# Loads of x^T and stores of the output issued by ACT instead of SP, in an attention over 4096 memory slots

## The chip, the cores and the metric

One core of a Trainium2 chip runs the whole program in one launch. The metric is the device time in microseconds. An engine here is PE (TensorE, matrix products), DVE (VectorE), ACT (ScalarE), POOL (GpSimd) or SP (SyncE, which only issues transfers). ACT can issue transfers too, on a queue of its own.

## The reference, cut to what matters

`x` is 8192 tokens of 128 numbers. The first layer attends to a memory of 4096 slots, the second is a gated feed-forward block with 512 hidden columns.

```
q      = x @ Wq.T + bq
scores = q @ keys.T / sqrt(128)                 # 8192 x 4096
probs  = softmax(scores)
attn   = (probs @ values) @ Wo.T + bo
x1     = layernorm(x + attn)
h      = silu((x1 @ w1.T) * s1) * ((x1 @ w2.T) * s2)
h      = gelu((h @ h1.T) * sh1)
h      = gelu((h @ h2.T) * sh2)
out    = layernorm(x1 + (h @ w3.T) * s3)
```

The keys, values and the updated memory of the attention layer are not returned; only `out` is.

## The kernel before, in words

**Pairs and frames.** The attention takes the tokens in 32 pairs (`PAIRS`) of tiles of 128 rows. Time is cut into frames, one per pair: `frames` writes out the first four and the last four, and a loop of two frames per pass runs twelve times for the 24 between. Each engine has its own function `frame(f, par)`, whose steps `t` (16 per frame, on PE, ACT and POOL) or `j` (8 per frame, on DVE and SP) set the order of its work; between engines only semaphores order anything. One step `j` is two steps `t`.

**One pair's way.** PE projects q of pair f+1 at t = 8 of frame f (`q_project`, L951, from the buffer `x_in`, which holds x^T of one pair). ACT and DVE turn it into a high and a low part (`q_high_part` L592, `q_low_part` L762). PE makes the scores of a tile, 512 slots a step, with three products of high and low parts (L998 to L1000). DVE moves each piece of 1024 scores from PSUM to `rows` and takes its maximum (L812); ACT takes the exponential in place (`exp_piece`, L613); DVE transposes blocks of 32 by 32 in place (L779). Then SP sends the piece over to `slot_p`, so that the slots come to lie on the partitions: `send` (L377) has four DMAs for a piece, each from 32 partitions to 32, of 4 KB each. A pair has 8 pieces, so 32 DMAs of 128 KB. That is the **exchange**.

**Behind the exchange.** From t = 14 of the next frame on, 16 steps long, ACT rounds the probabilities to 16 bit (`high_part`, L622) and POOL makes the low part (L542), into a ring of 8; the first high part of a pair waits for all eight pieces of its exchange (L620). PE multiplies them with the values (`add_values`, L972 to L977), from the frame after. So pair f-2's values run beside pair f's scores.

**What SP does in a frame.** `slot_p` has room for two pairs: SP may begin pair f's exchange (piece 5 in the frame, `j` = 5) when POOL has done the low parts of pair f-2. In front of each piece it waits for DVE's transposition. Between the pieces it sends two more DMAs: behind piece `j` = 3 it stores the output sum of pair f-3 (`store_output`, L249: `o_sum` to `o_scratch`, 128 partitions of 1 KB), and behind `j` = 6 it waits until q of pair f+1 is projected and loads x^T of pair f+2 into `x_in` (L447, 128 partitions of 1 KB).

```
exchange(p, par if j > PIECES else 1 - par, tile, k)
if j == 3 and valid(f - 3, PAIRS):
    stage.store_output(sp, f - 3)
if j == 6 and valid(f + 2, PAIRS):
    sp.wait_ge(q_projected, f + 2)
    load_x(f + 2)
```

**What ACT does in a frame.** A high part in each of the 16 steps, the exponential of a piece in every second one, q's high part at t = 8, the first half of the output sum at t = 1 (L238). From frame 3 to 27 it also loads 226 columns of the feed-forward weights at t = 3 (L650, 113 KB, on its own queue) and rounds them at t = 13 (L653). DVE makes the output sum early in the frame (L244), when the store before it has landed.

**Behind the attention** the feed-forward block takes 16 blocks of 512 tokens; SP loads `o_scratch` and `x` for it and stores the result. The last three stores of output sums stand there, in SP's code behind its frames.

Of the kernel before, what the change touches and what calls it, by code (L numbers as in the profile page):

```python
# [27 lines left out]
P = 128  # L28
# [7 lines left out]
PAIRS = TOKENS // (2 * P)  # L36
# [40 lines left out]
def is_step(index, step):  # L77

    return isinstance(index, int) and index == step
# [9 lines left out]
def valid(index, end):  # L89

    return not isinstance(index, int) or 0 <= index < end
# [160 lines left out]
def layers(nc, stage, hold, xT, wqT, bq, kT, vT, woT, bo, scale_cols, w_raw, den, keys, rows, out_rows):  # L252
# [6 lines left out]
    def sb(name, shape, dt):  # L259
        return ctx.enter_context(nc.sbuf_tensor(name, shape, dt))  # L260
# [7 lines left out]
    x_in = sb("x_in", [P, 2 * P], FP32)  # L268
# [25 lines left out]
    x_loaded, q_projected, q_high, q_split = map(sem, ("x_loaded", "q_projected", "q_high", "q_split"))  # L294
# [28 lines left out]
    def turned_piece(f, j):  # L323


        if j == 0:
            return f - 1, 0, PIECES - 1
        if j <= PIECES:
            return f - 1, 1, j - 1
        return f, 0, j - PIECES - 1  # L330

    def part_step(f, t, lag):


        return (f - 1, t - lag) if t >= lag else (f - 2, t + STEPS - lag)

    def value_halves(f, t):


        step = t - V_STEP + STEPS * f if isinstance(f, int) else -1  # L340
        return (step,) if 0 <= step < HALVES else ()

    def checking(f):

        return not isinstance(f, int) or 0 <= f - FIRST_CHECK < CHECKS
# [97 lines left out]
    def _(sp):  # L443
        def load_x(pair):
            if is_step(pair, 1):
                sp.wait_ge(warmed, 1)
            sp.dma_start(x_in[:, :], xT[:, bass.ds(pair * 2 * P, 2 * P)]).then_inc(x_loaded, 16)  # L447

        load_x(0)
        sp.dma_start(wq[:, :], wqT).then_inc(wq_loaded, 16)  # L450
# [14 lines left out]
        def exchange(p, pp, tile, k):  # L465


            sp.wait_ge(turned, 8 * p + 4 * tile + k + 1)
            if tile == 0 and k == 0:
                if is_step(p, 1):  # L470
                    sp.wait_ge(v_split, HALVES)
                    sp.wait_ge(k_split, K_PARTS)
                at_least(sp, split, 16 * p - 16)
            send(sp, pp, tile, k)

        def frame(f, par):
            for j in range(2 * PIECES):
                p, tile, k = turned_piece(f, j)
                if valid(p, PAIRS):
                    exchange(p, par if j > PIECES else 1 - par, tile, k)  # L480
                if j == 3 and valid(f - 3, PAIRS):
                    stage.store_output(sp, f - 3)
                if j == 6 and valid(f + 2, PAIRS):
                    sp.wait_ge(q_projected, f + 2)
                    load_x(f + 2)

        frames(sp, frame)

# [98 lines left out]
    def _(act):  # L587
# [36 lines left out]
        def frame(f, par):  # L624
            for t in range(STEPS):
                p, s = part_step(f, t, T_LAG)
                if valid(p, PAIRS):
                    high_part(p, 1 - par if t >= T_LAG else par, s)
                if t == 8 and valid(f + 1, PAIRS):
                    q_high_part(f + 1, 1 - par)  # L630
                if t % 2 == 0:
                    tile, k = (1, t // 2) if t < 8 else (0, (t - 8) // 2)
                    if valid(f - tile, PAIRS):
                        exp_piece(f - tile, tile, k)
                if is_step(f, 0) and t == 9:
                    act.wait_ge(v_sum_ready, 1)
                    nc.scalar.activation(wo_size, wo, ACT.Abs, scale=v_sums[:, PIECES:]).then_inc(wo_sized, 1)
                for n in value_halves(f, t):
                    act.wait_ge(v_made, n + 1)
                    nc.scalar.activation(half_piece(v_hi_flat, n), o_ps[:, n % 2, :], ACT.Copy).then_inc(v_high, 1)  # L640
                    if n == 0:
                        act.wait_ge(k_split, K_PARTS)
                    nc.scalar.activation(half_piece(v_raw, n), o_ps[:, n % 2, :], ACT.Copy).then_inc(v_copied, 1)
                if t == 1 and valid(f - 3, PAIRS):
                    if is_step(f, 3):
                        act.wait_ge(unscale_ready, 1)
                    stage.output_half(act, f - 3, 1 - par)
                if t == 3 and checking(f):
                    at_least(act, w_rested, f - FIRST_CHECK)
                    act.dma_start(w_check, w_raw[:, bass.ds((f - FIRST_CHECK) * CHECK_COLS, CHECK_COLS)]).then_inc(check_loaded, 16)  # L650
                if t == 13 and checking(f):
                    act.wait_ge(check_loaded, 16 * (f - FIRST_CHECK) + 16)
                    nc.scalar.activation(check_part(f), w_check, ACT.Copy).then_inc(stage.w_rounded, 1)  # L653
                if is_step(f, PAIRS - 4) and t == 0:
                    for b in range(2):
                        act.wait_ge(stage.o_stored, 16 * 2 * (b + 1))
                        stage.load_o(act, b, b)
# [523 lines left out]
```

## Time and profile before

| | |
|---|---|
| median of 3 runs | 1123.45 us (1122.45 to 1124.76) |
| the profiled execution | 1123.78 us |
| its span | 1122.1 us |
| PE busy | 1081.3 us, 96% of the span |
| DVE busy | 968.3 us, 86% |
| ACT busy | 905.3 us, 81% |
| POOL busy | 642.1 us, 57% |
| exchange DMAs (L377) issued by SP | 1016 of 128 KB, median 2.4 us to landing |
| loads of x^T (L447) and stores of the sum (L249) | 32 and 32 of 128 KB, median 2.4 and 2.1 us |

Busy is the time in which an engine works on an instruction; issuing a DMA or waiting doesn't count. The attention fills the span to about 750 us, and the feed-forward block the rest. The DMA engines are busy for eight or nine tenths in the attention and for one tenth behind it. TensorE's granted clock is full but for the first and a middle stretch of a few microseconds.

### The profile page before, as it was taken

The page shows a single profiled execution, that of the slowest core. Times are in us where ns is not written, and L with a number is a line of the kernel's source. Part 1 is how long each engine was busy: PE and PEld are TensorE (multiplying, and loading weights), DVE is VectorE, ACT ScalarE, POOL GpSimd, SP SyncE. Part 2 cuts the span into 40 slices and gives each one's busy share as a digit, 9 for nine tenths or more (in the row PEclk, how much of TensorE's full clock was granted, in tenths as well). Part 3 has the DMA queues.
Part 4 walks back from the last instruction along what each step waited for, and adds up shares of the span by engine and source line. Part 5 has one row for each costly group of instructions (what it writes and reads, how often), then busy time and mean ns, then how long its engine had stood idle before and what let it go on. Part 6 is the DMA issues. An engine that isn't in the chain of part 4 may idle for free.

```text
span 1122.1 us, 20046 instructions
## 1 busy us (share of the span) xinstructions
PE 1081.3 (96%) x5324; PEld 770.6 (69%) x5324; DVE 968.3 (86%) x1806; ACT 905.3 (81%) x1609; POOL 642.1 (57%) x615
## 2 busy tenths in 40 slices
PE   7899999999999999999999999979999999999996
PEld 5666666666666666666666666636888888888875
DVE  6988998998899989988999899887788887888884
ACT  6788788788888887888888878788788888878883
POOL 0487788788888787878887888760211121121110
PEclk9999999999999999999999999999999999999999
DMA  6888888988889889898898988891011011011000
GB/s 207 199 192 197 198 198 205 208 198 201 209 201 205 200 204 207 199 200 209 200 209 198 212 200 188 192 262 53 1 56 29 28 53 31 28 29 55 11 12 27
DMA packets 83941, 165.89 MB, mean 148 GB/s; under 512 B 19648, under 2 KB 47808, under 8 KB 83776
## 3 DMA queue, kind: packets, MB, share of 16 engines
q1 hardware_dynamic: 79632, 160.97, 60.4%
q10 hardware_dynamic: 4272, 4.47, 1.5%
q8 instruction: 18, 0.29, 0.1%
q14 instruction: 19, 0.16, 0.0%
HBM read 22.76 MB, written 8.39 MB: 28 GB/s over the span
## 4 chain that ended last, share of the span: by engine, by line
PE 36%; SPq 15%; ACT 13%; issue 10%; DVE 9%; POOL 8%; DMA 7%; ACTq 1%; DVEq 0%; POOLq 0%
SPq L377 14%; PE ring L1045 12%; PE ring L1046 12%; POOL pT L542 7%; ACT rows L613 7%; DMA slot_p<-rows 6%; ACT pT L622 5%; DVE rows L812 3%; DVE rows L779 3%; PE o_ps L1045 1%; PE o_ps L1046 1%; PE s_ps L1000 1%; PE s_ps L998 1%; PE s_ps L999 1%; PE o_ps L972 1%
## 5 line engine op out<-in xcount | busy, mean ns | idle before, releaser
L542 POOL TENSOR_TENSOR pT<-slot_p,pT 128x512 f16<-128x512 f32 x482 | 545.7, 1166 | 130.5 <-ACT pT L622 130.5
L622 ACT ACTIVATE pT<-slot_p 128x512 f16<-128x512 f32 x512 | 296.5, 617 | 72.5 <-DMA slot_p<-rows 60.3
L812 DVE TENSOR_SCALAR_CACHE_REDUCE rows<-s_ps 128x1024 f32<-128x1024 f32 x256 | 308.6, 1205 | 51.8 <-DMA slot_p<-rows 34.7
L779 DVE STREAM_TRANSPOSE rows<-rows 128x1024 f32<-128x1024 f32 x256 | 316.7, 1238 | 9.2 <-ACT rows L613 5.4
L613 ACT ACTIVATE rows<-rows,bias 128x1024 f32<-128x1024 f32 x256 | 291.7, 1140 | 12.6 <-DVE bias L820 12.0
L998 PE MATMUL s_ps<-keys,q_buf 128*128 128x512 f32 x512 | 249.6, 487 | 6.0 <-DVE rows L812 4.0
L972 PE MATMUL o_ps<-pT,v_hi 128*128 128x512 f16 x512 | 197.5, 386 | 18.5 <-POOL pT L542 11.2
L1000 PE MATMUL s_ps<-keys,q_buf 128*128 128x512 f32 x512 | 202.5, 396 | 0.0
L999 PE MATMUL s_ps<-keys,q_buf 128*128 128x512 f32 x512 | 201.3, 393 | 0.0
L975 PE MATMUL o_ps<-pT,v_lo 128*128 128x256 f16 x1024 | 196.1, 273 | 0.0
L977 PE MATMUL o_ps<-pT,v_hi 128*128 128x512 f16 x512 | 194.6, 380 | 0.0
L164 POOL TENSOR_TENSOR var_eps<-moments,eps 128x4 f32<-128x4 f32 x32 | 6.4, 199 | 312.8 <-DVE moments L185 312.8
L975 PEld LDWEIGHTS o_ps<-pT,v_lo 128*128 128x128 f16 x1024 | 101.1, 99 | 84.2 <-issue 0.6
L1045 PE MATMUL ring<-keys,w_all 128*128 128x512 f32 x384 | 153.3, 399 | 1.0 <-ACT gate L669 0.9
L1046 PE MATMUL ring<-keys,w_all 128*128 128x512 f32 x384 | 150.5, 392 | 0.0
L694 ACT ACTIVATE gelu<-ring,scales 128x512 f32<-128x512 f32 x128 | 87.8, 686 | 59.1 <-PE ring L1046 59.1
L972 PEld LDWEIGHTS o_ps<-pT,v_hi 128*128 128x128 f16 x512 | 49.3, 96 | 108.0 <-POOL pT L542 49.0
L998 PEld LDWEIGHTS s_ps<-keys,q_buf 128*128 128x128 f32 x512 | 97.0, 189 | 25.1 <-DVE rows L812 4.9
L1000 PEld LDWEIGHTS s_ps<-keys,q_buf 128*128 128x128 f32 x512 | 96.3, 188 | 22.7
L999 PEld LDWEIGHTS s_ps<-keys,q_buf 128*128 128x128 f32 x512 | 97.0, 189 | 17.5
L876 DVE TENSOR_TENSOR h_lo<-gelu,h_hi 128x512 fp32r<-128x512 f32 x128 | 81.9, 688 | 26.5 <-ACT h_hi L698 26.3
L1045 PE MATMUL ring<-h_hi,w_all 128*128 128x512 f32 x256 | 103.1, 403 | 0.3 <-ACT gate L669 0.3
(98 smaller groups left out, 1327.2 us busy)
## 6 DMA issues: line engine op xcount, KB each, us to landing
slot_p<-rows SPq DMA_DIRECT2D x1016, 128.0 KB, 2.4
x_in<-in_xT SPq DMA_DIRECT2D x32, 128.0 KB, 2.4
x_in<-in_x SPq DMA_DIRECT2D x16, 256.0 KB, 3.5
o_scratch<-o_sum SPq DMA_DIRECT2D x32, 128.0 KB, 2.1
out<-y_out SPq DMA_DIRECT2D x16, 256.0 KB, 2.4
o_in<-o_scratch SPq DMA_DIRECT2D x14, 256.0 KB, 3.2
z<-in_w_all ACTq DMA_DIRECT2D x25, 113.0 KB, 2.7
rows<-in_w_all SPq DMA_DIRECT2D x1, 2816.0 KB, 12.9
```

The source lines that it names most:

```text
L542: nc.gpsimd.tensor_tensor(halves(s % RING, 1), slots_first(pp, s), halves(s % RING, 0), ALU.subtract).then_inc(split, 1)
L613: nc.scalar.activation(s, s, ACT.Exp, bias=bias[:, tile:tile + 1], scale=SCALE, accum_out=den[:, bass.ds((2 * p + tile) * PIECES + k, 1)]) ...
L622: nc.scalar.activation(halves(s % RING, 0), slots_first(pp, s), ACT.Copy).then_inc(highed, 1)
L779: nc.vector.transpose(row_piece(tile, k), row_piece(tile, k)).then_inc(turned, 1)
L812: nc.vector.tensor_scalar(row_piece(tile, k), s_ps[:, j % 2, :], 1.0, None, ALU.mult, ALU.max, accum_out=part_max[:, tile, k:k + 1]).then_ ...
L972: nc.tensor.matmul(o_ps[:, pp, :], v_hi[:, 2 * s, :], pT[:, s % RING, 0, :], start=s == 0, stop=False, skip_group_check=True)
L975: nc.tensor.matmul(o_ps[:, pp, 0:2 * P], v_lo[:, 2 * s + c, :], pT[:, s % RING, c, 0:2 * P], start=False, stop=False, skip_group_check=True)
L998: nc.tensor.matmul(out, q_h, k_h, start=True, stop=False)
L999: nc.tensor.matmul(out, q_h, k_l, start=False, stop=False)
L1000: last = nc.tensor.matmul(out, q_l, k_h, start=False, stop=True)
L1045: nc.tensor.matmul(out, wh, hh, start=n == 0, stop=False)
L1046: last = nc.tensor.matmul(out, wh, hl, start=False, stop=final and not low_weights)
```

## The change

The two DMAs leave SP's frame and stand in ACT's, at t = 13: behind that step's high part, in front of the rounding of the weights' columns and of t = 14, where the first high part of a pair waits for its exchange. ACT waits for what SP waited for: `o_ready` for the store (inside `store_output`), `q_projected` for the load. SP keeps the first two loads of x^T and the last three stores of the sum.

```diff
@@ block.sync, load_x
-            sp.dma_start(x_in[:, :], xT[:, bass.ds(pair * 2 * P, 2 * P)]).then_inc(x_loaded, 16)
+            sp.dma_start(x_in[:, :], xT[:, pair * 2 * P:(pair + 1) * 2 * P]).then_inc(x_loaded, 16)
@@ block.sync, frame
                     exchange(p, par if j > PIECES else 1 - par, tile, k)
-                if j == 3 and valid(f - 3, PAIRS):
-                    stage.store_output(sp, f - 3)
-                if j == 6 and valid(f + 2, PAIRS):
-                    sp.wait_ge(q_projected, f + 2)
-                    load_x(f + 2)
@@ block.scalar, frame
+                if t == 13 and valid(f - 3, PAIRS):
+                    stage.store_output(act, f - 3)
+                if t == 13 and valid(f + 2, PAIRS):
+                    act.wait_ge(q_projected, f + 2)
+                    act.dma_start(x_in[:, :], xT[:, bass.ds((f + 2) * 2 * P, 2 * P)]).then_inc(x_loaded, 16)
                 if t == 13 and checking(f):
                     act.wait_ge(check_loaded, 16 * (f - FIRST_CHECK) + 16)
                     nc.scalar.activation(check_part(f), w_check, ACT.Copy).then_inc(stage.w_rounded, 1)
```

The order of SP's instructions in the second frame of the loop's body, behind piece `j` = 3, before. `x4` are the four DMAs of a piece; REGISTER_ALU and ISA rows work out what a wait compares with or where a DMA goes.

```order
L249 ISA
L249 DMA o_scratch<-o_sum 128x256
L468 REGISTER_ALU
L377 DMA slot_p<-rows 32x1024 x4
L468 ISA
L86 ISA
L377 DMA slot_p<-rows 32x1024 x4
L468 REGISTER_ALU
L377 DMA slot_p<-rows 32x1024 x4
L484 REGISTER_ALU
L447 ISA
L447 DMA x_in<-in_xT 128x256
```

The same place now, from piece `j` = 3 to the loop's branch:

```order
L377 DMA slot_p<-rows 32x1024 x4
L468 REGISTER_ALU
L377 DMA slot_p<-rows 32x1024 x4
L468 ISA
L86 ISA
L377 DMA slot_p<-rows 32x1024 x4
L468 REGISTER_ALU
L377 DMA slot_p<-rows 32x1024 x4
L468 REGISTER_ALU
L377 DMA slot_p<-rows 32x1024 x4
L368 REGISTER_ALU
L368 COMPARE_AND_BRANCH
```

SP's pieces follow each other with nothing between them.

ACT's instructions around t = 13 and 14 of a frame in the loop, now (the lines of the changed file are 5 lower than before up to this place: L617 is the high part L622, L608 the exponential L613):

```order
L608 ACTIVATE rows,den<-rows,bias 128x1024
L86 REGISTER_ALU
L617 ACTIVATE pT<-slot_p 128x2x256
L249 ISA
L249 DMA o_scratch<-o_sum 128x256
L650 ISA
L650 DMA x_in<-in_xT 128x256
L653 REGISTER_ALU
L653 ACTIVATE w_all<-z 128x226
L615 REGISTER_ALU
L86 ISA
L617 ACTIVATE pT<-slot_p 128x2x256
```

The two DMAs stand behind the sixteenth high part of one pair and in front of the wait (L615) of the first of the next. No other engine's order changes.

## Rows read from the trace of the kernel before

**Rows 1.** One frame: PE, PEld, DVE, ACT, POOL busy (count), clock, DMA share, GB/s.

```profile
401.37:423.54 22.17, 22.17 (x116) 15.14 (x115) 20.48 (x31) 18.73 (x35) 18.93 (x18) 1.00 0.87 199
```

**Rows 2.** ACT's timeline, q's conversion: start, duration, instruction, [idle before <- releaser].

```profile
83.87 0.48 ACT L592 ACTIVATE q_buf<-x_ps,bq_col 128x256 fp32r<-128x256 f32 x1 [1.76 <-PE x_ps L951]
...
221.18 0.47 ACT L592 ACTIVATE q_buf<-x_ps,bq_col 128x256 fp32r<-128x256 f32 x1 [1.30 <-PE x_ps L951]
...
401.37 0.47 ACT L592 ACTIVATE q_buf<-x_ps,bq_col 128x256 fp32r<-128x256 f32 x1 [1.31 <-PE x_ps L951]
...
423.54 0.47 ACT L592 ACTIVATE q_buf<-x_ps,bq_col 128x256 fp32r<-128x256 f32 x1 [1.62 <-PE x_ps L951]
...
446.28 0.47 ACT L592 ACTIVATE q_buf<-x_ps,bq_col 128x256 fp32r<-128x256 f32 x1 [1.28 <-PE x_ps L951]
...
626.30 0.47 ACT L592 ACTIVATE q_buf<-x_ps,bq_col 128x256 fp32r<-128x256 f32 x1 [1.29 <-PE x_ps L951]
...
695.84 0.48 ACT L592 ACTIVATE q_buf<-x_ps,bq_col 128x256 fp32r<-128x256 f32 x1 [1.22 <-PE x_ps L951]
```

**Rows 3.** PE's timeline, the held-up values' matmul.

```profile
436.70 0.39 PE L972 MATMUL o_ps<-pT,v_hi 128*128 128x512 f16 x1 [0.50 <-POOL pT L542]
```

**Rows 4.** POOL's and ACT's timelines: waits before low and first high parts.

```profile
425.88 5.65 POOL L542 TENSOR_TENSOR pT<-slot_p,pT 128x512 f16<-128x512 f32 x5 [1.59 <-ACT pT L622]
...
433.13 0.63 ACT L622 ACTIVATE pT<-slot_p 128x512 f16<-128x512 f32 x1 [2.70 <-DMA slot_p<-rows]
...
454.97 0.63 ACT L622 ACTIVATE pT<-slot_p 128x512 f16<-128x512 f32 x1 [1.69 <-DMA slot_p<-rows]
```

**Rows 5.** The chain of waits, 405 to 435 us: start, duration, what.

```profile
411.19 0.59 SPq L377
...
411.89 0.53 SPq L377
...
430.61 2.34 DMA slot_p<-rows
```

**Rows 6.** The page's chain by line; SP's waits in all (us, times, longest).

```profile
SPq L377 14%; PE ring L1045 12%; PE ring L1046 12%; POOL pT L542 7%; ACT rows L613 7%; DMA slot_p<-rows 6%; ACT pT L622 5%; DVE rows L812 3%; DVE rows L779 3%; PE o_ps L1045 1%; PE o_ps L1046 1%; PE s_ps L1000 1%; PE s_ps L998 1%; PE s_ps L999 1%; PE o_ps L972 1%
...
SPq L377 <- POOL pT L542: 15.2, 18, 1.3
```

**Rows 7.** SP's timeline, 405 to 430 us.

```profile
405.67 8.66 SPq L377 DMA_DIRECT2D slot_p<-rows  x12
414.58 0.36 SPq L447 DMA_DIRECT2D x_in<-in_xT  x1
415.06 12.95 SPq L377 DMA_DIRECT2D slot_p<-rows  x20
428.30 0.36 SPq L249 DMA_DIRECT2D o_scratch<-o_sum  x1
428.77 1.79 SPq L377 DMA_DIRECT2D slot_p<-rows  x3
```

**Rows 8.** ACT's timeline with its queue's issue, 414 to 418 us.

```profile
414.38 0.34 ACTq L650 DMA_DIRECT2D z<-in_w_all  x1
...
416.44 1.14 ACT L622 ACTIVATE pT<-slot_p 128x512 f16<-128x512 f32 x2
```

**Rows 9.** DMA views of 428:436, 440:445, 414:418; queues (packets, MB, share), issues (landing).

```profile
q1 hardware_dynamic: 696, 1.62, 87.6%
slot_p<-rows SPq DMA_DIRECT2D x13, 128.0 KB, 2.3
...
q1 hardware_dynamic: 394, 1.07, 100.4%
slot_p<-rows SPq DMA_DIRECT2D x9, 128.0 KB, 3.4
...
q10 hardware_dynamic: 144, 0.12, 11.2%
```

**Rows 10.** Line 377's issues by ACT: duration min/median/max in ns.

```profile
L377 ACTq DMA_DIRECT2D slot_p<-rows x8: 601/818/1352, 737.8 to 744.4; - x8
```

## The prediction

> **What bounds the kernel now.** I first read one frame of the loop as a window between two of ACT's conversions of q. From 401.37 to 423.54 us PE is busy for all of its 22.17 us at the full clock, while DVE, ACT and POOL are busy for 18.7 to 20.5 us [rows 1]. So a frame costs at least 22.17 us, and what can be won is only what stands above that. The starts of the conversions of q give the pace [rows 2]: 22.17 us from 401.37, but 22.74 us from 423.54. Over 18 frames, from 221.18 to 626.30, two frames take 405.12 / 9 = 45.01 us, against 2 x 22.17 = 44.34: **0.67 us per two frames is above PE's pace**.
>
> Where PE loses it stands in PE's timeline: the values' matmul of 436.70 was held up for 0.50 us by POOL's low part (L542) [rows 3]. Who held POOL up? POOL's first low part of a pair follows ACT's first high part (L622) at 433.13, and that had waited 2.70 us for the exchange to land [rows 4]. The exchange's last DMA was issued at 430.61 and took 2.34 us to land [rows 5]. So the path is: SP's queue of 32 exchange DMAs, a landing, ACT, POOL, PE. The chain of waits gives SP's exchange 14% of the span, more than any other line [rows 6].
>
> How full is SP? Twenty exchange DMAs take 12.95 us, 0.65 each, as do others whatever else runs [rows 7]. Beside the 32 of a pair, SP sends one load of x^T and one store. Between pairs SP is free: in all it waits 15.2 us in 18 places for POOL, 1.3 us at most [rows 6]. That wait ends by PE's own pace, not by SP's: POOL sat idle for 1.59 us for ACT at 425.88, and ACT for 1.62 us for PE's q at 423.54 [rows 2, 4]. So what SP saves inside a pair's exchange brings its end forward, and isn't handed on to the next start.
>
> **The change, part by part.**
>
> *Taken from SP.* The load: the exchange ends an issue at 405.67 + 8.66 = 414.33 and begins the next at 415.06, a hole of 0.73 us. The store: 415.06 + 12.95 = 428.01 to 428.77, 0.76 us [rows 7]. Between two groups of exchange DMAs with nothing between them the hole is 411.89 - (411.19 + 0.59) = 0.11 us [rows 5]. The load is therefore worth 0.62 and the store 0.65: **1.27 us per pair**, both ahead of the DMA that ACT's first high part waits for. That is 0.60 more than the 0.67 that PE lacks.
>
> *Given to ACT.* Two issues, 0.36 and 0.36 to 0.42 us on SP [rows 7], with two waits that were met long ago: the sum of output f-3 was made at the start of the same frame, and the projection of q is what ACT converted five steps before. I cost them at nothing, for two reasons. ACT idles 2.70 us right behind that place (1.69 in the other frame of a body) [rows 4]. And ACT's queue issues ahead of its arithmetic: the DMA of the weights' columns went out at 414.38, though it stands in the program between the two conversions that run from 416.44, so at least 2 us ahead [rows 8]. If that cover went, the price would be some 1.1 us, issued from 430.43, still over before a landing at about 432.
>
> *New: two queues at once.* The moved DMAs now lie in ACT's queue, leaving 2 to 5 us before SP's last exchange DMA, and their 256 KB share the DMA engines with the exchange. Before, they stood in SP's own queue and the exchange paid for them with a slot. The price is the least certain term. Nearest rows: while SP is alone its exchange DMAs land in 2.3 us and fill 87.6% of the engines; some microseconds behind the weights' DMA on ACT's queue they land in 3.4 us, and the engines are full at 100.4% [rows 9]. So one DMA of 113 KB can cost 1.1 us. The bounds for two moved ones are 0 (SP no later than alone) and 2 x 1.1 = 2.2 us. By engine time, the 113 KB took 11.2% of 4 us = 0.45 us [rows 9], so 256 KB take 1.02; with 12% of the engines free for some 4 us about 0.5 is left when the last DMA goes out, with none free all 1.02. I take 0.8 us, between the two and nearer the full state, since twice as much arrives at once as in that row.
>
> A rule of the Trainium skill, in DMA: Bandwidth & Descriptors, section Issuing engines are not separate DMA queues, speaks against the change: DMAs of all issuers run on the same 16 engines, and a second issuer saves only the sequencer's time, usually small beside the DMA. By that rule, the gain is the 1.27 us of issue at best and no data moves faster; the trace agrees with the first half, and here issue is no small part, since 32 slots of 0.65 us nearly fill the frame.
>
> *Not moved.* PE, DVE and POOL keep their order. The bytes are the same. The store leaves within some 3 us of where it did (428.30) and only has to land before the next frame's sum. x^T is loaded some 10 us earlier, just behind the projection that frees its buffer, and is needed a frame later. Both stay hidden. The stores of the last three pairs stay with SP.
>
> *The sum.* The last exchange DMA leaves 1.27 us earlier and lands 0.8 later: 0.47 us of the 0.67 come back, and 0.20 stay, as the wait of PE for POOL.
> - Nine loop bodies from 221.18 to 626.30: 9 x 0.47 = 4.2 us.
> - The six frames from 83.87 to 221.18 take 137.31 us, 4.29 over PE's pace [rows 2]. Entering the loop is in it; I take half, 2.1 us.
> - The three frames from 626.30 to 695.84 take 69.54 us, 3.03 over [rows 2]. DVE has the first block's residual there; I take a third, 1.0 us.
> - Behind that SP's stores mostly stay: nothing.
>
> In all 7.3 us. The profiled execution took 1123.78 us; 1123.78 - 7.3 = 1116.5. The median shown is 0.33 below that execution, so 1116.2 against it; I write **1116.5**.
>
> **The rivals.**
>
> *All of the stall goes.* If the late landing is 0.6 us or less, the 1.27 covers the 0.67. Then 9 x 0.67 = 6.0, three quarters of the 4.29 (3.2) and half of the 3.03 (1.5): 10.7 us, 1113. For it: by engine time it can be 0.5, and SP now rests longer between pairs, so that each exchange starts on empty engines. Against it: the 3.4 us behind a single 113 KB DMA.
>
> *It lands as late as it leaves early.* At 1.27 us, just over the 1.1 of the one measured burst, nothing is left: 1123. Another road to the same is that ACT, not the exchange, begins the pair late, but the 2.70 us of idle time speak against that.
>
> *Slower: the two queues hold the exchange back more than its slots did.* The place is the last four exchange DMAs of a pair, right behind the burst, and the point from which it decides is 1.27 us of added time. At the bound of 2.2 us PE would wait 2.2 - 0.60 = 1.6 us per body in place of 0.67: 0.93 x 12 bodies = 11 us, 1135. A milder form is that issues slow each other: near 740 us, where ACT and SP both send the exchange, ACT's eight issues took 601 to 1352 ns against the usual 590 [rows 10]. If ACT's two issues took 0.4 us each from SP, 0.8 of the 1.27 would be gone; with 0.8 of late landing PE would wait 1.0, 0.33 more than now, x 12 = 4 us, 1128. Against that: the weights' single issue of 0.34 us runs beside SP's, whose slots stay 0.65 [rows 7, 8]. By Perfetto Trace Analysis in the Trainium skill, section DMA Instruction — HWDGE (DVE, Sync), issuers take a lock on one generator of descriptors, and the wait for it is part of an issue's time; by that the milder form would hold for each of the two issues.
>
> *The change doesn't reach the path*, because SP only waits longer for POOL: 1123. That holds for what it saves between pairs, but the two slots stand inside the pair.
>
> **How the numbers follow.** A measurement of this kernel can tell about 0.2%, 2.2 us, from no change. My forecast (0.5 to 1.0 us of late landing) has 0.38, all of the stall gone 0.28: faster 0.66. Landing as late as it leaves early 0.14 and not reaching the path 0.06: same 0.20. Slower 0.14, most of it in the milder form. The range goes from 1111.5, a little beyond all of the stall gone, to 1125, which leaves out the larger part of the slower case: about 5% below and 12% above.
>
> **What would show it.** Right: between conversions of q 22.2 us in nearly every frame; PE's wait for POOL's L542 at most 0.3 us per body; no hole in SP's exchange inside a pair, and SP's waits for POOL between pairs longer by over 1 us each; ACT's two DMAs some microseconds ahead of its first high part; exchange DMAs behind them landing in about 3.1 us. Wrong: slots of SP above 0.65 us beside ACT's issues; landings of 3.6 us or more at the end of a pair with the pace still at 45 us per two frames; or PE's stall unchanged though the exchange lands over 1 us earlier, which would make ACT or POOL the holder, not SP.

## The result, and the profile after

Five runs of the kernel before have a median of 1124.06 us (1122.45 to 1124.76), five of the changed kernel one of 1117.74 us (1116.99 to 1118.10). The ratio is 0.9937 (95%: 0.9926 to 0.9949): the change makes the kernel faster by 0.63%, three times the 0.2% that the prediction took for the least a measurement can tell. 1116.5 was predicted, with a range that holds the measured time. The profiled execution took 1118.10 us, against 1123.78 before.

The head of the page after. The span is 5.7 us shorter; no engine has less to do by more than 2.4 us, so what went is mostly waiting:

```profile
span 1116.4 us, 20012 instructions
PE 1078.9 (97%) x5324; PEld 770.3 (69%) x5324; DVE 972.3 (87%) x1806; ACT 903.0 (81%) x1609; POOL 642.2 (58%) x615
```

**Where the time went** is read from ACT's timeline after, at the conversions of q that answer to [rows 2] (L587 is L592 before). A body is one pass of the loop, two frames:

```profile
84.20 0.48 ACT L587 ACTIVATE q_buf<-x_ps,bq_col 128x256 fp32r<-128x256 f32 x1 [1.76 <-PE x_ps L951]
...
220.15 0.48 ACT L587 ACTIVATE q_buf<-x_ps,bq_col 128x256 fp32r<-128x256 f32 x1 [1.30 <-PE x_ps L951]
...
398.39 0.47 ACT L587 ACTIVATE q_buf<-x_ps,bq_col 128x256 fp32r<-128x256 f32 x1 [1.31 <-PE x_ps L951]
...
420.48 0.47 ACT L587 ACTIVATE q_buf<-x_ps,bq_col 128x256 fp32r<-128x256 f32 x1 [1.63 <-PE x_ps L951]
...
443.12 0.47 ACT L587 ACTIVATE q_buf<-x_ps,bq_col 128x256 fp32r<-128x256 f32 x1 [1.29 <-PE x_ps L951]
...
621.99 0.48 ACT L587 ACTIVATE q_buf<-x_ps,bq_col 128x256 fp32r<-128x256 f32 x1 [1.32 <-PE x_ps L951]
...
690.99 0.48 ACT L587 ACTIVATE q_buf<-x_ps,bq_col 128x256 fp32r<-128x256 f32 x1 [1.75 <-PE x_ps L951]
```

| stretch | before | after | saved | predicted |
|---|---|---|---|---|
| up to the first of these | 83.87 | 84.20 | -0.33 | 0 |
| six frames | 137.31 | 135.95 | 1.36 | 2.1 |
| eighteen frames (nine bodies) | 405.12 | 401.84 | 3.28 | 4.2 |
| three frames | 69.54 | 69.00 | 0.54 | 1.0 |
| behind | 426.26 | 425.41 | 0.85 | 0 |
| sum | | | 5.70 | 7.3 |

The same frames as windows after: PE, PEld, DVE, ACT, POOL busy (count), clock, DMA share, GB/s. Two frames of about 22.1 us stand beside one of 22.64, at full clock; [rows 2] had 22.17 and 22.74:

```profile
376.34:398.39 22.05, 21.90 (x114) 14.53 (x113) 20.62 (x32) 18.17 (x35) 17.96 (x18) 1.00 0.90 210
398.39:420.48 22.09, 22.09 (x116) 15.06 (x115) 20.25 (x30) 18.62 (x36) 18.94 (x18) 1.00 0.85 200
420.48:443.12 22.64, 22.32 (x116) 14.89 (x115) 20.84 (x34) 18.61 (x36) 18.36 (x18) 1.00 0.93 208
```

**SP.** Its timeline after, for the stretch of [rows 7]. The exchange DMAs, 32 of one pair and the first of the next, form one row with neither a load nor a store in it:

```profile
406.28 25.76 SPq L377 DMA_DIRECT2D slot_p<-rows  x38
```

**ACT.** Its timeline after. The two DMAs are issued at 421.76 and 422.31, though they stand in the program behind the high part of 426.33 (t = 13): 4.6 and 4.0 us ahead of it, and 4.5 and 3.9 us ahead of SP's last exchange DMA of that pair (426.25, below). The first high part waits 2.74 us, as it did before (2.70, [rows 4]). The exponential behind it follows with no gap:

```profile
421.76 0.37 ACTq L249 DMA_DIRECT2D o_scratch<-o_sum  x1
422.31 0.34 ACTq L650 DMA_DIRECT2D x_in<-in_xT  x1
...
426.33 0.62 ACT L617 ACTIVATE pT<-slot_p 128x512 f16<-128x512 f32 x1
426.85 0.38 ACT L653 ACTIVATE w_all<-z 128x226 f32 x1
429.96 0.63 ACT L617 ACTIVATE pT<-slot_p 128x512 f16<-128x512 f32 x1 [2.74 <-DMA slot_p<-rows]
...
430.50 1.14 ACT L608 ACTIVATE rows<-rows,bias 128x1024 f32<-128x1024 f32 x1
```

**The landing.** The chain of waits after, for the place of [rows 5], where the last exchange DMA took 2.34 us to land. It now takes 3.53:

```profile
425.62 0.59 SPq L377
426.25 3.53 DMA slot_p<-rows
```

The DMA view after of 423 to 427 us, queues as packets, MB, share of 16 engines, and the issues with their landing. ACT's queue holds 21.3% and SP's 77.9%, together 99.2%:

```profile
q1 hardware_dynamic: 284, 0.77, 77.9%
...
q10 hardware_dynamic: 288, 0.26, 21.3%
...
slot_p<-rows SPq DMA_DIRECT2D x7, 128.0 KB, 3.5
```

**PE.** Its timeline after: the matmul of [rows 3] waits 0.32 us instead of 0.50.

```profile
433.54 0.39 PE L972 MATMUL o_ps<-pT,v_hi 128*128 128x512 f16 x1 [0.32 <-POOL pT L537]
```

The waits between 221 and 622 us (us in total, times, longest), of the kernel before:

```profile
ACT pT L622 <- DMA slot_p<-rows: 39.6, 18, 2.7
PEld o_ps L972 <- POOL pT L542: 26.9, 75, 1.1
...
PE o_ps L972 <- POOL pT L542: 5.4, 9, 0.7
```

and of the changed kernel:

```profile
ACT pT L617 <- DMA slot_p<-rows: 40.7, 18, 2.8
...
PEld o_ps L972 <- POOL pT L537: 18.2, 56, 0.8
...
PE o_ps L972 <- POOL pT L537: 1.2, 4, 0.4
```

PE's matmuls wait for POOL 4 times in place of 9, 1.2 us in place of 5.4, and its weight loads 18.2 us in place of 26.9. ACT waits for the exchange as long as before: what SP no longer takes, the landing takes. In the whole span, SP's own wait for POOL grew:

```profile
SPq L377 <- POOL pT L537: 39.8, 24, 2.2
```

That is 24.6 us more than the 15.2 of [rows 6]: 1.27 us in some twenty pairs would be 25. (A second row of SP's waits for POOL, at line 86, has 6.3 us in 5 places before and 8.7 in 6 after.) What SP saves inside a pair it gives to the pause between pairs.

### The profile page after: what moved, and what is told of

The parts are those of the page before. It is cut to its first block, busy times and chain, and to the rows that moved or that the text cites. A ratio compares the mean times of both kernels' runs of the same rounds, so it can differ in the third digit from the quotient of the medians.

```text
span 1116.4 us, 20012 instructions
## 1 busy us (share of the span) xinstructions
PE 1078.9 (97%) x5324; PEld 770.3 (69%) x5324; DVE 972.3 (87%) x1806; ACT 903.0 (81%) x1609; POOL 642.2 (58%) x615
## 4 chain that ended last, share of the span: by engine, by line
PE 47%; issue 11%; ACT 10%; POOL 9%; DVE 8%; SPq 7%; DMA 6%; ACTq 1%; POOLq 0%; DVEq 0%
PE ring L1045 13%; PE ring L1046 12%; POOL pT L537 9%; SPq L377 7%; ACT rows L608 5%; DMA slot_p<-rows 5%; ACT pT L617 3%; PE s_ps L1000 3%; PE s_ps L998 3%; PE s_ps L999 3%; PE o_ps L972 3%; PE o_ps L975 3%; PE o_ps L977 3%; DVE rows L779 2%; DVE rows L812 2%
## 5 line engine op out<-in xcount | busy, mean ns | idle before, releaser
L617 ACT ACTIVATE pT<-slot_p 128x512 f16<-128x512 f32 x512 | 296.5, 617 | 75.2 <-DMA slot_p<-rows 70.5
L812 DVE TENSOR_SCALAR_CACHE_REDUCE rows<-s_ps 128x1024 f32<-128x1024 f32 x256 | 309.4, 1209 | 38.4 <-PE s_ps L1000 20.3
L608 ACT ACTIVATE rows<-rows,bias 128x1024 f32<-128x1024 f32 x256 | 291.6, 1139 | 5.5 <-DVE bias L820 5.3
```

What stands on the lines that cost most here:

```text
L608: nc.scalar.activation(s, s, ACT.Exp, bias=bias[:, tile:tile + 1], scale=SCALE, accum_out=den[:, bass.ds((2 * p + tile) * PIECES + k, 1)]) ...
L617: nc.scalar.activation(halves(s % RING, 0), slots_first(pp, s), ACT.Copy).then_inc(highed, 1)
L812: nc.vector.tensor_scalar(row_piece(tile, k), s_ps[:, j % 2, :], 1.0, None, ALU.mult, ALU.max, accum_out=part_max[:, tile, k:k + 1]).then_ ...
```

## The experiments

The theory to be tested: SP's 32 slots and what stands between them, the landing, ACT, POOL and PE form one path; ACT's issues cost nothing where they stand; the moved bytes cost the landing. All kernels were read in one way, by the timelines of SP and ACT. Each number is a mean over the seventeen pairs 10 to 26 of the loop: **start**, the first exchange issue behind the conversion of q ahead of it; **slots**, first to last exchange issue; **landing**, last issue to ACT's first high part; **path**, their sum; **pace**, us per frame. In eleven of the twelve kernels the high part starts 0.19 us behind the landing of the last exchange DMA, so that the column does tell of the landing. In g1_all_sp it doesn't, as its section shows.

| kernel | start | slots | landing | path | pace |
|---|---|---|---|---|---|
| before | 8.10 | 21.06 | 2.53 | 31.69 | 22.51 |
| after | 7.90 | 19.80 | 3.65 | 31.35 | 22.31 |
| e1_store | 8.50 | 20.42 | 3.13 | 32.05 | 22.62 |
| e2_load | 7.94 | 20.44 | 2.87 | 31.25 | 22.25 |
| e3_behind | 8.30 | 19.83 | 3.70 | 31.83 | 22.85 |
| e4_between | 7.88 | 19.82 | 2.77 | 30.47 | 22.08 |
| f1_small | 7.88 | 19.79 | 2.70 | 30.37 | 22.08 |
| f2_small_sp | 8.02 | 21.05 | 2.52 | 31.59 | 22.44 |
| f3_small_behind | 7.90 | 19.79 | 3.05 | 30.74 | 22.34 |
| f4_double | 7.89 | 19.94 | 4.03 | 31.86 | 22.51 |
| g1_all_sp | 8.41 | 19.83 | 3.53 | 31.77 | 22.47 |
| g2_store6 | 8.16 | 20.49 | 3.31 | 31.96 | 22.58 |

The runs f1_small, f2_small_sp and f3_small_behind leave out seven eighths of each store and load, so that their output isn't the reference's; they are for the time alone. The kernels of one letter ran on one chip, each against the kernel before on that chip: 1125.14 us (e), 1126.00 (f), 1125.45 (g).

### Only the store moved

```diff
@@ SP, frame
-                if j == 3 and valid(f - 3, PAIRS):
-                    stage.store_output(sp, f - 3)
@@ ACT, frame
+                if t == 13 and valid(f - 3, PAIRS):
+                    stage.store_output(act, f - 3)
```

> Only the store of the output sum moves to ACT at t = 13; the load of x^T stays between SP's pieces. Theory A (SP's slots are won inside a pair's exchange, and the moved DMAs' landing gives most of it back): the last exchange DMA of a pair leaves 0.65 us earlier (20.6 us behind the first in place of 21.25) and lands some 0.5 us later; a tenth of a microsecond per pair is left, 1121 to 1123.5 us. Rival B (the gain of the change is the store's alone, since it stood right ahead of the last piece): about 1118. Rival C (it is the load's alone): 1124, no change.

Measured: 1126.23 us, ratio 1.0009 (1.0000 to 1.0018). This is no gain, and none of the expected 1121 to 1123.5: a miss. Half of the slots' saving is there (20.42 in place of 21.06), but the landing takes back 0.60 of the 0.64, and the exchange starts 0.40 later. The time is what rival C forecast for this run.

### Only the load moved

```diff
@@ SP, frame
-                if j == 6 and valid(f + 2, PAIRS):
-                    sp.wait_ge(q_projected, f + 2)
-                    load_x(f + 2)
@@ ACT, frame
+                if t == 13 and valid(f + 2, PAIRS):
+                    act.wait_ge(q_projected, f + 2)
+                    act.dma_start(x_in[:, :], xT[:, bass.ds((f + 2) * 2 * P, 2 * P)]).then_inc(x_loaded, 16)
```

> Only the load of x^T moves to ACT at t = 13; the store stays between SP's pieces. Theory A: 0.62 us earlier, some 0.5 us later in landing, 1121 to 1123.5 us. Rival B (the store's alone): 1124, no change. Rival C (the load's alone): about 1118.

Measured: 1116.45 us, ratio 0.9919 (0.9904 to 0.9934). The load alone brings at least all of the gain. Theory A's 1121 to 1123.5 is missed here too; rival C's forecast of both runs was the nearest. Its reason, that a load is cheap and a store dear, is put to the test by the last experiment. The slots are as long as in the first experiment, but the landing is 2.87 and not 3.13, and the start is early. SP's timeline and ACT's show how: ACT's load leaves at 422.95, SP's store at 425.76, with the last piece's four exchange DMAs behind the store, and the high part waits only 2.04 us. The DMA views of 423.6 to 425.7 us and of 426.2 to 428.2 have the landings on either side of the store's place: 3.1 us ahead of it, 2.4 behind it.

```profile
403.63 21.84 SPq L377 DMA_DIRECT2D slot_p<-rows  x32
425.76 0.34 SPq L249 DMA_DIRECT2D o_scratch<-o_sum  x1
```

```profile
422.95 0.34 ACTq L650 DMA_DIRECT2D x_in<-in_xT  x1
...
430.60 0.63 ACT L619 ACTIVATE pT<-slot_p 128x512 f16<-128x512 f32 x1 [2.04 <-DMA slot_p<-rows]
```

```profile
slot_p<-rows SPq DMA_DIRECT2D x3, 128.0 KB, 3.1
...
slot_p<-rows SPq DMA_DIRECT2D x4, 128.0 KB, 2.4
```

### Both on ACT, behind its first high part

Against the changed kernel:

```diff
@@ ACT, frame
                     high_part(p, 1 - par if t >= T_LAG else par, s)
+                if t == 14 and valid(f - 3, PAIRS):
+                    stage.store_output(act, f - 3)
+                if t == 14 and valid(f + 2, PAIRS):
+                    act.wait_ge(q_projected, f + 2)
+                    act.dma_start(x_in[:, :], xT[:, bass.ds((f + 2) * 2 * P, 2 * P)]).then_inc(x_loaded, 16)
...
-                if t == 13 and valid(f - 3, PAIRS):
-                    stage.store_output(act, f - 3)
-                if t == 13 and valid(f + 2, PAIRS):
-                    act.wait_ge(q_projected, f + 2)
-                    act.dma_start(x_in[:, :], xT[:, bass.ds((f + 2) * 2 * P, 2 * P)]).then_inc(x_loaded, 16)
```

> Both DMAs on ACT, but behind the first high part of a pair (t = 14), so that they go out only when the pair's exchange has landed, near the next pair's start. Theory A: the last exchange DMA leaves 20.0 us behind the first as in the change, and now lands in 2.5 us again in place of 3.6; PE's wait for POOL's first low parts goes, q's conversions stand 22.1 us apart in every frame, 1110 to 1114 us. Rival D (what is left of PE's stall is ACT's or POOL's own, not the late landing): 1117 to 1119, with the landing at 2.5 us. Rival E (the burst does the same harm wherever it lies, since the exchange runs nearly without a gap): landing at 3.3 us or more at the pair's end, 1117 to 1120.

Measured: 1132.83 us, ratio 1.0065 (1.0052 to 1.0079), slower, and outside all three forecasts, none of which gave ACT's issues a price. Two things show. The landing is 3.70, as rival E said, though the burst now leaves at the beginning of an exchange and not near its end. And ACT's issues are in the way. Its timeline:

```profile
436.63 0.63 ACT L617 ACTIVATE pT<-slot_p 128x512 f16<-128x512 f32 x1 [1.70 <-DMA slot_p<-rows]
436.79 0.37 ACTq L249 DMA_DIRECT2D o_scratch<-o_sum  x1
437.33 0.35 ACTq L628 DMA_DIRECT2D x_in<-in_xT  x1
437.81 1.15 ACT L608 ACTIVATE rows<-rows,bias 128x1024 f32<-128x1024 f32 x1 [0.56 <-issue]
```

The exponential, which in the changed kernel ran on the heels of the high part, stands idle for 0.56 us for issue. A gap of 0.56 in each pair's round of two frames is 0.28 per frame; the pace of 22.85 lies some 0.34 above the 22.5 that other kernels have at a path of 31.7 to 31.9.

### Both on SP, where it waits for POOL anyway

Against the kernel before:

```diff
@@ SP, frame
             for j in range(2 * PIECES):
+                if j == 5 and valid(f - 3, PAIRS):
+                    stage.store_output(sp, f - 3)
+                if j == 5 and valid(f + 2, PAIRS):
+                    sp.wait_ge(q_projected, f + 2)
+                    load_x(f + 2)
                 p, tile, k = turned_piece(f, j)
                 if valid(p, PAIRS):
                     exchange(p, par if j > PIECES else 1 - par, tile, k)
-                if j == 3 and valid(f - 3, PAIRS):
-                    stage.store_output(sp, f - 3)
-                if j == 6 and valid(f + 2, PAIRS):
-                    sp.wait_ge(q_projected, f + 2)
-                    load_x(f + 2)
```

> Both DMAs stay on SP, but stand together in front of the first piece of a pair (j = 5), where SP waits for POOL's low parts. ACT issues nothing more than before. Theory A (only what lies between the first and the last exchange DMA counts, and SP has over 1 us to spare between pairs): 20.0 us from first to last, landing in 2.5 us, 1110 to 1115 us. Rival F (SP's issues in all are the bound, or the second queue is what helps): 1123 to 1125, as before. In between if the wait for POOL is shorter than the 1.27 us of the two slots, so that the first piece starts late.

Measured: 1111.99 us, ratio 0.9881 (0.9866 to 0.9896), the best of all the kernels that compute the whole. The slots are 19.82 as in the change, the landing is 2.77 (2.53 before), and the path falls by 1.22. So theory A holds and rival F is out. SP's timeline: both issues lie in the pause between two pairs, the 32 of a pair follow each other in 20.59 us.

```profile
401.43 0.42 SPq L249 DMA_DIRECT2D o_scratch<-o_sum  x1
402.13 0.35 SPq L447 DMA_DIRECT2D x_in<-in_xT  x1
402.98 20.59 SPq L377 DMA_DIRECT2D slot_p<-rows  x32
```

Its frames, with the columns of [rows 1]. PE is busy in all of both, in 21.99 and 22.17 us, so that 22.08 is what PE alone needs on the average; the 22.17 of [rows 1] was the longer kind of frame:

```profile
373.11:395.10 21.99, 21.99 (x116) 14.96 (x115) 20.23 (x30) 18.68 (x36) 18.68 (x18) 1.00 0.89 210
395.10:417.27 22.17, 22.17 (x116) 15.14 (x115) 21.01 (x33) 18.62 (x36) 18.65 (x18) 1.00 0.88 204
```

### The bytes or the issues?

Four kernels ask what makes the landing late. In the first three, the store and the load inside the frames move 16 partitions and not 128. The first is the changed kernel with this:

```diff
-        sp.dma_start(self.o_dram[:, bass.ds(p * 2 * P, 2 * P)], self.o_sum[:, :]).then_inc(self.o_stored, 16)
+        sp.dma_start(self.o_dram[0:16, bass.ds(p * 2 * P, 2 * P)], self.o_sum[0:16, :]).then_inc(self.o_stored, 16)
...
-                    act.dma_start(x_in[:, :], xT[:, bass.ds((f + 2) * 2 * P, 2 * P)]).then_inc(x_loaded, 16)
+                    act.dma_start(x_in[0:16, :], xT[0:16, bass.ds((f + 2) * 2 * P, 2 * P)]).then_inc(x_loaded, 16)
```

> The change, but every moved load and every store of the sum takes 16 partitions of 1 KB in place of 128 (the feed-forward block reads its attention part from x^T instead, so the output leaves the attention out): ACT issues as often, an eighth of the bytes. Theory G (it is the bytes on ACT's queue that make the exchange land late): the last exchange DMA leaves 20.0 us behind the first and lands in 2.6 to 3.0 us, as where SP sends both between the pairs; frames of 22.1 us, 1110 to 1113 us. Rival H (it is the issuing from a second queue as such, or ACT's time for it): landing at 3.3 us or more, 1116 to 1118.

Measured: 1111.99 us, ratio 0.9868 (0.9852 to 0.9884). As theory G said, the landing falls from 3.65 to 2.70 and the pace to PE's own 22.08.

The second is the kernel before, with the same small DMAs on SP:

```diff
-                sp.dma_start(x_in[:, :], xT[:, bass.ds(pair * 2 * P, 2 * P)]).then_inc(x_loaded, 16)
+                sp.dma_start(x_in[0:16, :], xT[0:16, bass.ds(pair * 2 * P, 2 * P)]).then_inc(x_loaded, 16)
```

> The kernel before, with the same loads and stores cut to 16 partitions, on SP in their old places. Theory I (on SP it is the slot that costs, not the bytes): 21.25 us from first to last exchange DMA as before, 1122 to 1125 us. Rival J (it is the bytes): landing at 2.3 us or less and frames of 22.1 us, 1112 to 1116. Between the two if a DMA of 16 partitions has a shorter slot.

Measured: 1121.99 us, ratio 0.9958 (0.9941 to 0.9975). The time is at the lower edge of theory I's range. The slots stay at 21.05, the landing at 2.52. On SP it is the two places in the queue that cost most; the bytes are worth 4.0 us by the medians, against the 13.2 that clearing both places brought in e4_between. On ACT it is the bytes.

The third is the kernel with both behind ACT's first high part, with small DMAs:

```diff
+                if t == 14 and valid(f + 2, PAIRS):
+                    act.wait_ge(q_projected, f + 2)
+                    act.dma_start(x_in[0:16, :], xT[0:16, bass.ds((f + 2) * 2 * P, 2 * P)]).then_inc(x_loaded, 16)
```

> Both DMAs on ACT behind the first high part, as in the slower run, but with 16 partitions. Theory K (that run lost time twice: 1 us by late landing at the pair's end, and 0.66 us because ACT's second high part of a pair waits behind two issues): now the landing is 2.6 to 3.0 us, and the first high part to PE's first values stays at 4.2 us against 3.6; together 1112 to 1118 us. Rival L (all of its loss was the late landing): 1110 to 1113, with 3.6 us from the first high part to PE's values.

Measured: 1118.10 us, ratio 0.9927 (0.9910 to 0.9943). The bytes are all but gone and the path is 30.74, yet the pace is 22.34 and not 22.08. The time lies 0.1 us above theory K's range and the landing of 3.05 just above its 3.0; rival L is out. What is left is ACT's issue time, in its timeline:

```profile
428.11 0.40 ACTq L249 DMA_DIRECT2D o_scratch<-o_sum  x1
428.68 0.35 ACTq L629 DMA_DIRECT2D x_in<-in_xT  x1
429.16 1.15 ACT L609 ACTIVATE rows<-rows,bias 128x1024 f32<-128x1024 f32 x1 [0.58 <-issue]
```

The first of the three has the same DMAs ahead of ACT's wait and not behind it, and is 6.1 us faster. The price of two issues without cover is 0.56 to 0.58 us of ACT, and about 0.26 us per frame.

The fourth is the changed kernel, with the store sent twice, the second time to a tensor that nobody reads:

```diff
         sp.dma_start(self.o_dram[:, bass.ds(p * 2 * P, 2 * P)], self.o_sum[:, :]).then_inc(self.o_stored, 16)
+        sp.dma_start(self.o_dram2[:, bass.ds(p * 2 * P, 2 * P)], self.o_sum[:, :]).then_inc(self.o_stored, 16)
```

> The change with every store of the sum sent twice, the second time to another buffer in memory: 384 KB per frame from ACT's queue at t = 13 in place of 256. Theory G: the last exchange DMA lands 0.3 to 0.6 us later still, about 4.0 to 4.3 us, 1120 to 1126 us. Rival M (lateness doesn't grow with the bytes, it is a state that any burst brings about): 3.6 us as in the change, 1117 to 1119.

Measured: 1124.92 us, ratio 0.9990 (0.9979 to 1.0002). The landing rises from 3.65 to 4.03, the slots from 19.80 to 19.94: 0.5 us more of path for 128 KB, and the gain is gone. From 32 KB on ACT's queue (2.70) to 256 (3.65) to 384 (4.03) the landing rises by 0.4 us per 100 KB and by 0.3. So the more is moved, the later the landing, and rival M is out. Bytes and packets grow together in these runs (the view of 423 to 427 us above has 288 packets for the 0.26 MB of ACT's two DMAs), so that they don't tell the one from the other. And here ACT's issues do slow SP's: in f4_double, the 56 of SP's exchange issues between 230 and 620 us that overlap one of ACT's store or load took 611 ns in the mean; in the changed kernel the 42 such issues took 575, as all of them there do.

### Everything on SP, and the store at another place

If a second queue is what delays the exchange, then it should run free with ACT's queue silent. This kernel is that with both on SP in the pause, and the weights' columns there as well:

```diff
@@ SP, frame, ahead of the store at j == 5
+                if j == 5 and checking(f):
+                    at_least(sp, w_rested, f - FIRST_CHECK)
+                    sp.dma_start(w_check, w_raw[:, bass.ds((f - FIRST_CHECK) * CHECK_COLS, CHECK_COLS)]).then_inc(check_loaded, 16)
@@ ACT, frame
-                if t == 3 and checking(f):
-                    at_least(act, w_rested, f - FIRST_CHECK)
-                    act.dma_start(w_check, w_raw[:, bass.ds((f - FIRST_CHECK) * CHECK_COLS, CHECK_COLS)]).then_inc(check_loaded, 16)
```

> Store, load and also the load of the weights' columns on SP, all three in front of the first piece of a pair (j = 5); ACT's queue issues nothing in the frames. Theory A: landing is 2.5 us at the end of every pair (it was 2.6 and 2.95 with the weights' columns on ACT's queue), but PE was already at its pace of 22.1 us per frame, so 1109 to 1113 us. Rival N (three slots are longer than SP's wait for POOL, so the exchange starts some 0.3 us late and PE waits again): 1114 to 1118.

Measured: 1123.29 us, ratio 0.9978 (0.9968 to 0.9988), outside both forecasts. The late start that the rival named is there (8.41 in place of 7.88). SP's timeline shows the three DMAs one behind the other, and the exchange directly behind them:

```profile
407.62 0.44 SPq L480 DMA_DIRECT2D z<-in_w_all  x1
408.27 0.36 SPq L249 DMA_DIRECT2D o_scratch<-o_sum  x1
408.90 0.34 SPq L447 DMA_DIRECT2D x_in<-in_xT  x1
409.48 20.59 SPq L377 DMA_DIRECT2D slot_p<-rows  x32
```

The 3.53 of the table look like a late landing, but aren't one. The DMA view of 409.5 to 430 us, which holds that exchange, gives the median of its 32 landings:

```profile
slot_p<-rows SPq DMA_DIRECT2D x32, 128.0 KB, 2.3
```

The last exchange DMA of a pair lands in 2.35 us on the average of the seventeen pairs, earlier than in e4_between (2.58): that part of theory A holds. ACT's timeline shows what the first high part (L625) waited for instead. In front of it in the program stands the rounding of the weights' columns (L653), and their load now leaves SP only at 430.33, behind the exchange's last issue, and no longer at t = 3, ten steps ahead of the rounding:

```profile
429.52 0.63 ACT L625 ACTIVATE pT<-slot_p 128x512 f16<-128x512 f32 x1
432.55 0.39 ACT L653 ACTIVATE w_all<-z 128x226 f32 x1 [2.40 <-DMA z<-in_w_all]
433.01 0.63 ACT L625 ACTIVATE pT<-slot_p 128x512 f16<-128x512 f32 x1
```

The same in the waits between 221 and 622 us, where no wait of L625 is left:

```profile
ACT w_all L653 <- DMA z<-in_w_all: 41.9, 18, 2.6
```

The high part comes 1.17 us behind the landing in place of 0.19, and this 0.98 is a wait that the edit itself made. Without it the path would be 31.77 - 0.98 = 30.79, and the pace about 22.04 by what the other kernels have (22.25 at 31.25, 0.46 per microsecond), which is PE's own; that is an estimate, no run has it. So 369 KB on SP's own queue just ahead of the exchange don't make it land late, where 256 KB on ACT's queue do (e3_behind).

The last kernel asks why the load alone did better than the store alone. It is the one that moved only the load, with SP's store not behind piece `j` = 3, near the end of an exchange, but behind `j` = 6, near its beginning:

```diff
-                if j == 3 and valid(f - 3, PAIRS):
+                if j == 6 and valid(f - 3, PAIRS):
                     stage.store_output(sp, f - 3)
```

> Load of x^T on ACT at t = 13 as in the run that gained most of the two single ones, and SP's store one position earlier in the pair's exchange: behind j = 6, where the load's slot was, in place of j = 3, right ahead of the last piece. Theory O (the slot of a short transfer in SP's queue right ahead of the last piece lets the DMA engines catch up, so that the last piece lands in 2.6 us in spite of ACT's burst): landing now 3.0 us or more, 1120 to 1126 us. Rival P (a load on ACT's queue is cheap and a store is dear, wherever SP's own stands): landing 2.6 to 2.9 us, 1115 to 1118.

Measured: 1124.81 us, ratio 0.9995 (0.9985 to 1.0005), against 0.9919 with the store at `j` = 3. The bytes, queues and counts are the same; the slots too (20.49 and 20.44). The landing is 3.31 in place of 2.87 and the start 8.16 in place of 7.94. So theory O holds and rival P is out. Here the eight exchange DMAs issued from 426 to 430.6 us, behind the burst and with no place between them, land in 3.0 us (median); in e2_load it was 3.1 ahead of the store and 2.4 behind it. A place in SP's queue that holds a short transfer lets the DMA engines catch up: it helps if it stands between the burst and the end of the exchange, and is wasted if it stands ahead of the burst.

## Why the prediction was right, and which term was off

**What bounds the kernel: held, with a floor 0.09 too high.** In the table, the pace follows the path: from 31.25 to 32.05 us of path it rises from 22.25 to 22.62, 0.46 us per frame for each microsecond (g1_all_sp is on this line too, since its path has ACT's wait for the weights' columns in it). A pair's path lies in a round of two frames, so one half is what it should be. At 30.4 us it stands at PE's 22.08, where that line would lie lower. Only the two kernels with ACT's issues behind the first high part lie off this line. Against 22.08, PE lacked 45.01 - 44.16 = 0.85 us per body and not 0.67.

**The slots taken from SP: 1.27 predicted, 1.26 measured** (21.06 - 19.80), and 24.6 us longer waits for POOL between pairs, as the prediction said. Its reading that SP waits for POOL 15.2 us in all, 1.3 at most, left out the row of line 86 (6.3 us, longest 1.9); nothing in the sum rests on it. That the saving stands inside the pair, and is worth something only there, is what the kernel with both on SP in the pause shows: the same slots, all of the gain. "The change doesn't reach the path" is out.

**ACT's issues at nothing: held.** The queue ran 4.0 and 4.6 us ahead of the arithmetic in front of it in the program; at least 2 had been expected. The cover is needed: without it the price is 0.56 us.

**The late landing: the term that was mis-sized.** 0.8 was taken, 3.65 - 2.53 = 1.12 us was measured. The prediction took engine time (1.02 us if no engine is free) and put it down a little for the 12% it thought free. With the view of 423 to 427 us at 99.2%, none was free. So the exchange alone gave 1.26 - 1.12 = 0.14 us per pair, not 0.47: at this point the rival "lands as late as it leaves early" was all but true.

**What made up for it was not foreseen.** The exchange starts 0.20 us earlier behind q (7.90 in place of 8.10). 0.14 + 0.20 is 0.34 us per body, and the nine bodies gave 3.28 / 9 = 0.36. The cause of the earlier start is argued and not shown: in the span's waits, DVE waited for its own rows' last landing (L812) 34.7 us before and 15.4 after, so that its pieces, which SP sends, are made sooner; in the loop alone (221 to 622 us) they are 19.2 before, 8.1 after and 25.1 in e1_store, whose exchange starts at 8.50. No run takes this alone. So the closeness of 1116.5 to 1117.74 is in part luck: a saving that the prediction had no term for made up for most of what the landing cost beyond 0.8. With 0.14 us per pair alone, its own sum would give 7.3 x 0.14 / 0.47 = 2.2 us, about 1121.6, still inside its range. Two of its signs of being right failed: only every second frame takes the 22.1 us that it wanted in nearly every one (22.09 and 22.64 stand side by side), and the exchange DMAs behind the burst land in 3.5 us, not 3.1. One of its signs of being wrong, 3.6 us or more with the pace still at 45 us per two frames, was near: the table's landing is 3.65, the pace 44.65.

**The other stretches** were estimated by shares and came to 1.36 and 0.54 in place of 2.1 and 1.0, about the same factor as in the loop. The 0.33 lost ahead of them and the 0.85 us behind the attention are not explained by any run. For the latter a candidate stands in the trace before: for the 3.4 us from 739.4 the granted clock was 0.50 (the lower level, 1.2 GHz), with PE busy for 3.18 of them. In the trace of the changed kernel it was 0.50 only at the very end, where PE was idle.

**The rivals.** "All of the stall goes" was put at 1113 and needed a landing under 0.6 us later. It didn't come, but f1_small and e4_between show that it was right about what would follow: 1111.99 both. "Slower: the two queues" had its place right and its size wrong: 1.12 us, not 2.2, stays below the 1.27 from which it decides, and f4_double, at 1.50 later with slots 0.14 longer, is just at the turn (0.9990). For its milder form, slots lengthened by ACT's issues, the kernel gives no support: line 377's issues on SP have a median of 591 ns after and 590 before, and the slots are 19.80 us beside ACT's two issues and 19.82 without them (e4_between). Only three of ACT's issues lengthened them, in f4_double, by 0.14. By Perfetto Trace Analysis in the Trainium skill, section DMA Instruction — HWDGE (DVE, Sync), ACT's issues and SP's would have to wait for one lock; if they do, it doesn't show in a median, two issues beside 32.

The rule of DMA: Bandwidth & Descriptors in the Trainium skill, section Issuing engines are not separate DMA queues, did hold: one set of DMA engines serves both queues, and the bytes moved to ACT came back as 1.12 us of landing, against 1.26 of issue time. What it calls usually small was 0.63 us for each of the two DMAs here.

**Still open.** Why a burst of about 1 us of engine time on ACT's queue still costs 0.9 us at the end of an exchange twenty microseconds later (3.70 in e3_behind against 2.77 in e4_between) is argued from the lack of slack; none of the runs looks inside the engines. Nor is it shown whether the same bytes on SP's queue are harmless (g1_all_sp) because of the queue or because SP issues no exchange DMA for the 2 us that the three issues take. And the change, e2_load and e4_between were each measured against the kernel before, not against each other; the intervals of e4_between and the change don't touch, those of e2_load and the change do.

## What to carry to other kernels

Moving a DMA to another engine's queue takes its slot from the first, not its bytes from the engines: where a chain of transfers is issued back to back and its end is waited for, look for a pause of the same queue in which the short transfers cost neither, ahead of a second queue (0.9881 against 0.9937 here). Look first at who waits for each transfer that is moved: in g1_all_sp the weights' load, sent later, made ACT's first high part 0.98 us later than the exchange did. If there is no pause, leave one short transfer near the chain's end, behind the burst, and not ahead of it. And put an engine's issues where its next wait is longer than they are: two issues of 0.35 us cost nothing in front of a wait of 2.7 us, and 0.56 us behind it.

## What the runs showed of the hardware that was not expected

- A delay of the DMA engines fades only slowly under a queue that issues 128 KB every 0.64 us (20.59 us for 32). A burst on ACT's queue at the beginning of an exchange (e3_behind, 3.70) makes the high part as late as one near its end (3.65), against 2.53 to 2.87 where a pause or a short transfer of SP's stands behind the burst. In e3_behind the median is 3.7 us for the issues of 416 to 418 us, behind the burst, and 3.4 for those of 429.5 to 433.5, the last of the same exchange, with a load of the weights' columns in between. One place of a short transfer took the landing from 3.1 to 2.4 us (e2_load).
- 369 KB on SP's own queue, in three DMAs just ahead of an exchange, left its landings at 2.3 us (g1_all_sp).
- On SP, a DMA with 16 partitions takes the same place in the queue as one with 128: slots of 21.05 and 21.06 us.
- ACT's DMAs left up to 4.6 us ahead of the arithmetic that stands in front of them in the program, but the same issues blocked the next activation for 0.56 to 0.58 us where no wait covered them.
